# Queueing chunk 3's input ahead of chunk 2's rows, and scaling its K and V earlier on ScalarE, in an RWKV and SwiGLU layer

## What is computed

```python
xx = shift_by_one_step(x)
xk = x * time_mix_k + xx * (1.0 - time_mix_k)     # xv and xr alike
k, v, sr = xk @ Wk.T, xv @ Wv.T, sigmoid(xr @ Wr.T)
rwkv = sr * _wkv(-exp(time_decay), time_first, k, v)   # a recurrence over the steps
x = layernorm(x + rwkv @ Wo.T)
h = silu(x @ wg.T) * (x @ wu.T)                   # hidden size 768
x = layernorm(x + h @ wd.T)
```

## Time and profile before

| what | value |
|---|---|
| time, median of 3 runs | 301.95 us (301.76 to 302.52) |
| time of the profiled execution | 302.23 us |
| its span, first to last instruction | 300.3 us |
| TensorE busy | 274.7 us, 91% |
| VectorE busy | 260.9 us, 87% |
| ScalarE busy | 217.2 us, 72% |
| GpSimd busy | 190.5 us, 63% |
| mean granted TensorE clock | 0.958 |

### The profile page before, as it was taken

How to read it: one execution, slowest core, us unless ns; L and a number is a source line. 1 busy time by engine, 2 the same in 40 slices (tenths; PEclk the granted TensorE clock), 3 DMA queues, 4 the chain that set the end, 5 groups by cost and what they waited for, 6 DMA issues and landing times.

```text
span 300.3 us, 4239 instructions
## 1 busy us (share of the span) xinstructions
PE 274.7 (91%) x1250; PEld 202.6 (67%) x1250; DVE 260.9 (87%) x450; ACT 217.2 (72%) x386; POOL 190.5 (63%) x157
## 2 busy tenths in 40 slices
PE   7479769997699999999999999999999999999990
PEld 5335457744589467956896578757885689778890
DVE  5897498797669999999999998999999999888663
ACT  3569867167866698679876989579967883699373
POOL 3769964338996877588759866886764681334030
PEclk9959989997699999999999999999999999999996
DMA  7902200040030400122012201030102010102003
GB/s 246 346 3 70 71 3 0 0 141 2 10 95 2 123 18 32 42 70 70 0 70 73 71 0 70 9 96 0 70 1 71 0 70 2 35 2 71 0 3 109
DMA packets 13525, 16.26 MB, mean 54 GB/s; under 512 B 704, under 2 KB 11200, under 8 KB 13504
## 3 DMA queue, kind: packets, MB, share of 16 engines
q1 hardware_dynamic: 12816, 15.48, 16.1%
q10 hardware_dynamic: 688, 0.53, 0.6%
HBM read 11.81 MB, written 4.19 MB: 53 GB/s over the span
## 4 chain that ended last, share of the span: by engine, by line
PE 67%; ACT 9%; DVE 8%; POOL 7%; issue 3%; DMA 2%; DVEq 0%; SPq 0%; ACTq 0%; POOLq 0%
PE bank_a L1028 13%; PE bank_b L1028 12%; PE bank_a L1051 12%; PE bank_b L996 8%; PE bank_d L986 7%; PE bank_c L986 6%; PE bank_a L986 6%; POOL wts L346 4%; POOL dx L327 2%; DVE state L688 2%; ACT mix L457 2%; DMA xt<-xT 2%; PE bank_b L1005 2%; PE bank_c L1028 1%; DVE state L676 1%
## 5 line engine op out<-in xcount | busy, mean ns | idle before, releaser
L366 POOL TENSOR_TENSOR hlo<-hid,hhi 128x512 fp32r<-128x512 f32 (+1 forms) x36 | 52.1, 1451 | 33.6 <-ACT hhi L531 33.5
L333 POOL TENSOR_TENSOR mix<-mix,xt 128x512 f32<-128x512 f32 (+1 forms) x48 | 55.0, 1176 | 7.8 <-ACT mix L457 7.7
L346 POOL TENSOR_SCALAR wts<-gap,par 128x512 f32<-128x512 f32 (+1 forms) x18 | 35.3, 1960 | 21.4 <-DVE gap L656 20.4
L1051 PE MATMUL bank_a<-wd_r,hhi 128*128 128x256 f32 x192 | 47.0, 286 | 0.0
L1051 PE MATMUL bank_a<-wd_r,hlo 128*128 128x256 f32 x192 | 45.8, 279 | 0.0
L457 ACT ACTIVATE mix<-dx,par 128x512 f32<-128x512 f32 x48 | 31.3, 711 | 14.9 <-POOL dx L327 14.9
L1028 PE MATMUL bank_a<-x1hi,wg_r 128*128 128x512 f32 (+1 forms) x96 | 33.4, 430 | 6.6 <-ACT act L523 4.3
L779 DVE TENSOR_TENSOR hid<-bank_b,act 128x512 f32<-128x512 f32 (+1 forms) x48 | 30.8, 643 | 8.8 <-ACT act L523 4.1
L1051 PEld LDWEIGHTS bank_a<-wd_r,hhi 128*128 128x128 f32 x192 | 36.0, 188 | 2.3 <-issue 1.5
L1051 PEld LDWEIGHTS bank_a<-wd_r,hlo 128*128 128x128 f32 x192 | 36.0, 188 | 0.3 <-issue 0.2
L531 ACT ACTIVATE hhi<-hid 128x512 fp32r<-128x512 f32 (+1 forms) x54 | 31.0, 575 | 6.2 <-DVE hid L779 6.2
(11 more groups left out here) (103 smaller groups left out, 566.9 us busy)
## 6 DMA issues: line engine op xcount, KB each, us to landing
xt<-xT SPq DMA_DIRECT2D x7, 513.0 KB, 3.7
xrow<-x SPq DMA_DIRECT2D x7, 512.0 KB, 3.7
out<-y SPq DMA_DIRECT2D x6, 512.0 KB, 2.8
wg_i<-wg SPq DMA_DIRECT2D x1, 768.0 KB, 8.3
wu_i<-wu SPq DMA_DIRECT2D x1, 768.0 KB, 9.8
wd_i<-wd SPq DMA_DIRECT2D x1, 768.0 KB, 11.4
out<-y SPq DMA_DIRECT2D x3, 256.0 KB, 3.1
xt<-xT SPq DMA_DIRECT2D x2, 257.0 KB, 2.9
```

Source lines behind the costliest of these rows:

```text
L333: nc.gpsimd.tensor_tensor(mix[:, s, i, h, 0:n], mix[:, s, i, h, 0:n], xt[:, h, 0:n], ALU.add).then_inc(mixed, 1)
L346: nc.gpsimd.tensor_scalar(wts[:, OUT, h, 0:n], gap[:, h, 0:n], par[:, FIRST, h:h + 1], CAP, ALU.add, ALU.min).then_inc(out_arg_ready, 1)
L366: nc.gpsimd.tensor_tensor(hlo[:, m, 0:n], hid[:, m % NH, 0:n], hhi[:, m, 0:n].bitcast(f32), ALU.subtract).then_inc(hlo_ready, 1)
L1051: mm = nc.tensor.matmul(ffn[:, q, :], hp.bitcast(f32) if full else hp, w[:, m, :], start=(m == 0 and q % 2 == 0 and part is hhi), stop=(m ...
```

## The change

SyncE issues the load of chunk 3's transposed input before the load of chunk 2's rows. ScalarE scales the K and V tiles of chunk 3 (4 instructions) directly after the two `x1_high` copies of chunk 1, ahead of the last four exponentials of chunk 2; the two R tiles stay behind the exponentials. GpSimd's, VectorE's and TensorE's programs are as they were. The number of instructions on every engine is the same.

```diff
@@ -296,8 +296,8 @@
             load_xrow(0)
             load_xt(2)
             load_xrow(1)
+            load_xt(3)
             load_xrow(2)
-            load_xt(3)
             load_xt(4)
@@ -555,7 +555,7 @@
                 if isinstance(j, int) and j == 1:
                     scale_chunk(2, 0, [R])
                     first_norm(j, nxt)
-                    scale_chunk(3, s)
+                    scale_chunk(3, s, [R])
                     return
@@ -574,6 +574,8 @@
                     weights(j + 1, 0, range(2))
                 x1_high(j, 0)
                 x1_high(j, 1)
+                if isinstance(j, int) and j == 1:
+                    scale_chunk(3, 1, [K, V])
                 if nxt and not first(j):
                     weights(j + 1, 0, [OUT])
```

## The result

| | before | changed |
|---|---|---|
| median | 302.36 us (301.43 to 304.42, 9 runs) | 299.45 us (298.58 to 300.27, 9 runs) |
| profiled execution, time (span) | 302.23 (300.3) | 299.92 (298.1) |

The ratio is 0.9901, with a 95% interval from 0.9876 to 0.9926: 3.0 us less (0.0099 x 302.36), and the interval puts it between 2.2 and 3.7. The forecast was 299.1, with 3.0 us gained.

What follows compares the result with a forecast made beforehand. TensorE bounds the steady part, so only its earlier waits can gain: 2.71 us of ScalarE idle time, minus 0.1 for `shift`, plus 0.4 for the clock, gives 3.0 us and 299.1 us, range 297.4 to 300.7.

Steps and rivals of the forecast that it cites:

- The load: SyncE's `load_xt(3)`: issued at about 56.1 us instead of 59.74, 3.7 us in transit, landing at 59.8 (58.8 to 63.0).
- the two idle times: ScalarE's waits of 2.30 and 0.41 us for GpSimd's `wts` before `silu(1, 0)`; removing both was to gain 2.71 us.
- Part 3: ScalarE: four scalings of K and V fill the idle time, so `silu(1, 0)` starts at about 74.35 instead of 77.06.
- The charge of 0.1 us for `shift`: VectorE's small `shift` of norm 1, slowed by `dx` beside it: up to 0.4 us later, 0.1 charged (0 to 0.5).
- The scans beside the mixes: VectorE's two `scan_bb` beside GpSimd's K and V mixes: 0.54 us longer each, 1.1 together; nothing charged, 0.2 without cover.
- Behind round 2 nothing new is late.: GpSimd's mix of chunk 3 ends near 76.6, some 4.4 us earlier; VectorE's 1.80 us wait for `hlo` shrinks.
- The clock: TensorE's slow work behind its longer gap: 5.3 us instead of 6.1, a gain of 0.4 us (-0.4 to +1.5).
- Rival B: TensorE's clock comes back early, 1.5 us instead of 0.4: gain 4.1, 297.9 us; chance 0.17.
- The gap: TensorE, running tiles 0 and 1 sooner, stands still about 4.5 us before `act` of tile 0.
- C: Rival: the longer gap keeps TensorE's clock low for up to 10.3 us; gain 0.5 to 1.6, about 300.8 us; chance 0.12.
- D: Rival: the load comes no earlier or `out_arg` is held otherwise, so ScalarE idles as long; 301.9 us, chance 0.04.
- E: Rival: `dx` late, ending after 69.8, so scalings at ScalarE's queue head delay recurrence and `silu`; 304 with 2 us beyond; chance 0.05.

Runs made afterwards that it cites:

- load_only: The kernel before with only chunk 3's input load issued ahead of chunk 2's row load, ScalarE's order kept; ratio to the kernel before 0.9925.
- scalar_only: The changed kernel with chunk 3's load back in its old place, so only ScalarE's order is new; 302.07 us, ratio to the kernel before 1.0008.
- before_short_r: The kernel before, with GpSimd adding only 64 of 512 columns of chunk 3's two R tiles; ratio to the kernel before 0.9970.
- warm: The changed kernel, with TensorE repeating tile 1's last up product three times (12 matmuls) in its gap; 299.62 us, ratio to the kernel before 0.9912.
- change_again: The changed kernel itself, measured once more beside the other runs; 299.0 us against 301.82, ratio to the kernel before 0.9914.
- after: The first profile of the changed kernel, nothing further changed; profiled execution 299.92 us, ratio of the kernel to the one before 0.9901.
- r_behind_low: The changed kernel, with GpSimd mixing chunk 3's R tiles in round 2 behind all four low parts of chunk 1; ratio to the kernel before 0.9947.
- k_early: The changed kernel, with chunk 3's K tiles scaled after chunk 1's `rstd` and mixed directly behind `dx`; 297.47 us, ratio to the kernel before 0.9838.
- k_early_warm: As k_early, with TensorE also repeating tile 1's last up product once (4 matmuls) before its wait; 297.49 us, ratio to the kernel before 0.9840.

## Why the prediction was right, and where it was wrong

The time was right: 3.0 us forecast and 3.0 measured, 299.1 against 299.45. Part of that is luck, for the path that carries the gain was drawn through ScalarE and TensorE alone. Point by point:

- **The load.** Forecast at 56.1, landing at 59.8; measured 56.51 and, by the start of `dx`, 60.3, in an execution that runs 0.5 us late. Right. The rows of chunk 2 were hidden, right.
- **GpSimd's `out_arg`.** 64.0 forecast, 64.50 measured. Right, with the same 0.5. The pair took 4.42 us, not 4.05.
- **ScalarE.** The sum of the two idle times, 2.71 us; 2.95 measured from `x1hi` to silu. Right. That the reordering of ScalarE belongs to this gain was implied in Part 3, and is wrong: load_only has it all, since ScalarE has the same work in either order once nothing is waited for.
- **The charge of 0.1 us for `shift`.** It took 0.17 us at most; the charge was not needed.
- **The scans beside the mixes.** Forecast 1.8 us each, measured 1.95 and 1.64; `hid` of tile 0 started at 75.31, right behind its `act` (74.68 + 0.60), as forecast. The step that failed is the other side of it: the contention was costed for VectorE alone. GpSimd's mixes grew from 8.23 to 9.69 us, for which I had taken the old duration.
- **"Behind round 2 nothing new is late."** This step failed. The denominator sums were to come at 76.6, 4.4 us earlier, and came at 78.77, 2.2 earlier: 0.5 us of the difference from the late execution, 1.46 from the longer mixes, 0.2 from a start of the mixes that was forecast too early. TensorE was to run without a gap from 75.0 and waited 0.51 and 0.48 us. scalar_only and before_short_r show that GpSimd's chain was nearly level with ScalarE's already in the kernel before: the 1.80 us wait for `hlo` in the earlier trace rows stood there, and I read it as harmless because TensorE, at its low clock until about 84, was late enough itself not to wait for what came of it. And the wait did not shrink, as I had written, but was 1.83 us.
- **The clock.** The slow work was 3.4 us, not the 5.3 taken; by my sum that is worth 6.1 - 3.4 = 2.7, halved 1.35 us, not 0.4. The cost of the clock after the change was taken too high, and that of GpSimd's chain left out. Nothing of the 1.35 us arrived: TensorE restarted 2.38 us earlier (2.9 without the 0.5 of the late execution) and reached `attention_out(2)` 2.18 us earlier (2.7), as the waits for `hid` and `hlo` took the surplus. Rival B, with its short slow stretch, is what the clock did; it said that VectorE and GpSimd would let the gain through, and warm shows that they do not. The total came out right because the two errors nearly cancel.
- **The gap.** I expected 4.5 us and 3.52 were measured: the 16 matmuls of tiles 0 and 1 ran from 67.28 to 71.81, 4.5 us, where my 4.5 us of idle time before 75.0 let them end at 70.5.

Rivals C, D and E did not occur. For E nothing was tried: no kernel here had the load land late enough.

## What to carry to other kernels

When an idle time on one engine is about to be removed, follow the engine that caused it on to its next customers: here GpSimd made ScalarE wait once, and held VectorE with its later work as well, so a reordering that fed only ScalarE gained nothing (1.0008) and one that fed both gained 1.6% (0.9838). A wait that costs nothing in the trace before, only because the engine behind it is itself late (here at its low clock), is not slack that a faster chain can use. And two engines that slow each other down must both be costed, the one that is moved and the one it is moved beside.

## What the runs showed of the hardware

- Six mixes on GpSimd (128x512, two inputs) took 8.23 us beside a VectorE that stood still for 3.7 us of it, 8.63 with one `scan_bb` ahead of them and a VectorE still for 3.3 us (load_only), and 9.68 to 9.72 beside both (change_again, after, warm). Single mixes took 1.08 to 1.30 us, and 1.70 to 2.21 where they started while one of VectorE's scans was running: three of the six in change_again, and three in scalar_only, which has 9.69 us with its first `scan_bb` ahead of the mixes; two in load_only and before. Of two that met in load_only the one that had started first kept its time: the scan at 69.64 took 1.28 and the mix at 69.89 2.10; the mix at 75.27 took 1.28 and VectorE's scan at 75.42 2.22. From load_only to change_again the mixes lose 1.05 us and the two scans, 1.95 + 1.65 against 1.28 each, 1.04. VectorE's two low parts took 3.29 us beside two mixes (r_behind_low) and 1.28 with GpSimd idle (change_again).
- The granted clock did not fall in the k_early execution over a gap of 2.30 us, and fell in `after` and change_again over one of 3.52. In scalar_only it did not fall over 1.07 us, and read 0.76 for 84 to 90 us behind the 3.74 us wait. It fell over 1.34 us in the kernel before, and not over 1.37 in k_early_warm. Behind two waits of 0.54 and 0.60 us (67.4 and 68.9) it read 0.51 from 70 to 73.5 in scalar_only, and behind two of 0.54 and 0.61 it read 1.00 there in before_short_r. So the length of a wait alone did not decide whether it fell.
